# Sharing the square root, inverse and offset of two layer norms, and dividing half of the heads on ScalarE, in the combine stage of a graph network kernel

## The reference

```python
msgs = jnp.where(deg[:, None, None] > 0, agg, V)      # agg: weighted sums over a node's edges, each head over its denominator
out = msgs.reshape(N, H * D) @ Wo + bo
x1 = out + node_features
gnn = (x1 - mean(x1)) / jnp.sqrt(var(x1) + 1e-05) * gamma + beta
x = x + gnn + mix(xn)                                 # mix ends in a product with Wproj
x = x + ffn(layernorm(x))                             # the gate of ffn takes the second norm's rows
```

## Time and profile before

| | us |
|---|---|
| median of 3 runs | 1252.35 (1250.92, 1252.35, 1252.89) |
| the profiled execution, whole | 1250.91 |
| its span | 1249.2 |
| DVE in the combine: its first instruction to the gate's bias | 826.77 to 944.61 |

### The profile page before, as it was taken

How to read it: one execution, slowest core, us unless ns; L and a number is a source line. 1 busy time by engine, 2 the same in 40 slices (tenths; PEclk the granted TensorE clock), 3 DMA queues, 4 the chain that set the end, 5 groups by cost and what they waited for, 6 DMA issues and landing times. The chain is left out here.

```text
span 1249.2 us, 26412 instructions
## 1 busy us (share of the span) xinstructions
PE 1095.1 (88%) x7190; PEld 842.0 (67%) x7191; DVE 919.0 (74%) x1987; ACT 814.8 (65%) x2874; POOL 803.1 (64%) x835
## 2 busy tenths in 40 slices
PE   4999957999999999999999999968883599999992
PEld 3777734666767666767767676657872588888872
DVE  7787548899999999999999999859876323223230
ACT  3445400788888889898988888614673456666661
POOL 4777657777777777777777777117541356666661
PEclk9999965899999999999999999979995799999997
DMA  8333368888888888888888888258125633343444
GB/s 233 123 126 125 128 162 245 241 241 240 241 234 247 237 242 234 237 240 244 238 243 239 242 240 238 69 174 291 64 92 161 200 52 60 66 64 62 67 64 120
DMA packets 131578, 220.51 MB, mean 177 GB/s; under 512 B 24900, under 2 KB 89580, under 8 KB 131400
## 3 DMA queue, kind: packets, MB, share of 16 engines
q0 software_dynamic: 48832, 138.49, 41.3%
q1 hardware_dynamic: 82632, 80.63, 20.9%
HBM read 188.00 MB, written 34.25 MB: 178 GB/s over the span
## 5 line engine op out<-in xcount | busy, mean ns | idle before, releaser
L640 POOL DMA_INDIRECT KV<-kv,ixs x464 | 477.7, 1030 | 148.5 <-issue 135.6
L656 ACT ACTIVATE KV<-KV,WS 128x65 f32<-128x65 f32 x1728 | 434.0, 336 | 17.9 <-ACT RR L702 14.8
L769 PE MATMUL ps_o<-KV,PM 128*128 128x260 f32 x928 | 252.8, 395 | 20.3 <-DVE PM L888 13.9
L750 PE MATMUL ps_qe<-Q,PT 128*128 x1392 | 201.6, 284 | 5.6 <-DVE PT L856 5.1
L769 PEld LDWEIGHTS ps_o<-KV,PM 128*128 128x128 f32 x928 | 158.8, 190 | 60.6 <-DVE PM L888 29.1
L750 PEld LDWEIGHTS ps_qe<-Q,PT 128*128 128x128 bf16 x1392 | 137.1, 100 | 52.9 <-issue 10.1
L774 PE MATMUL ps_o<-ACC,ident 128*128 x464 | 158.5, 423 | 0.6 <-ACT ACC L682 0.6
L877 DVE TENSOR_TENSOR KV<-KV,ps_qe 128x512 f32<-128x512 f32 x232 | 149.8, 677 | 0.2
L870 DVE TENSOR_TENSOR KV<-KV,ps_u 128x1024 f32<-128x1024 f32 x116 | 140.3, 1209 | 8.8 <-DMA KV<-kv,ixs 8.8
L1547 POOL DMA_INDIRECT acc<-YG,DX x56 | 89.2, 1593 | 79.2 <-issue 49.0
L883 DVE TENSOR_REDUCE S<-KV 128x16 f32<-128x1024 f32 x116 | 138.8, 1197 | 1.1
(11 more groups left out here) (298 smaller groups left out, 1655.2 us busy)
## 6 DMA issues: line engine op xcount, KB each, us to landing
dlb<-dl_rows SPq DMA_DIRECT2D x116, 128.0 KB
W<-in_f_W_dram SPq DMA_DIRECT2D x16, 512.0 KB, 6.4
tyb<-ty_rows SPq DMA_DIRECT2D x116, 64.0 KB
KV<-kv,ixs POOLq DMA_INDIRECT x464
kv<-kvb SPq DMA_DIRECT2D x25, 258.0 KB, 2.4
xs_rows<-xs SPq DMA_DIRECT2D x25, 256.0 KB, 2.5
VB<-kv SPq DMA_DIRECT2D x5, 650.0 KB, 8.2
X<-in_x_dram SPq DMA_DIRECT2D x5, 640.0 KB, 10.8
```

Source lines behind the costliest of these rows:

```text
L640: pool.indirect_dma_start(kv[:, c % KR, n, :], None, d["kv"], bass.IndirectOffsetOnAxis(ap=T["ixs"][:, c % KR, n:n + 1], axis=0)).then_inc ...
L656: m = a.activation(part, part, ACT.Copy, scale=W[:, c % 2, s * H + h:s * H + h + 1])
L750: m = pe.matmul(T["ps_qe"][:, p % 3, k, :], T["PT"][:, h, (p % 2 * 2 + k) * P:(p % 2 * 2 + k + 1) * P], T["Q3"][:, bass.ds(at + n * C, C)] ...
L769: m = pe.matmul(T["ps_o"][:, p % RO, 0:A], PM[:, p // 2 % 2, p % 2 * 2 + k, :], kv[:, c % KR, 2 * x + k, C:KVW], start=(k == 0), stop=False)
```

## The change

Three things, all in the combine.

- Pass j has one square root, one inverse and one offset for both norms: of tile j for the first norm and of tile j - 4 for the second. The statistics move to tables indexed by pass (`mv2`, `rs2`, `nm2`: NT + 4 passes by two norms), so that one instruction takes both as two elements of a row. For passes that have one norm only it takes one element (`norms`). `deviations` waits for both variances.
- DVE's `message` takes heads 0 and 1 (128 elements a row). ACT gets a `message` for heads 2 and 3, two copies of 128x64 with a scale per row, issued last in its pass; those of tiles 0 and 1 come ahead of everything. PE's turn waits for both halves (`s_ma`).
- ACT's copies of tile 0 wait for `first_messages` on a semaphore of their own (`s_fm`).

```diff
+    s_fm, s_ma = sem("cb_first_sums"), sem("cb_messages_by_scalar")
...
+    NSTEP = NT + ST2
+
+    def norms(j):
+        return slice(0 if j < NT else 1, 2 if j >= ST2 else 1)
...
+    HV = 2
...
             def message(t):
                 wait(v, s_pv, 2 * (t // CT_))
-                v.tensor_tensor(VB[:, t, 0:C].rearrange("p (h d) -> p h d", h=H), acc3[:, t, :].rearrange("p (h d) -> p h d", h=H)[:, :, 0:D],
-                                dn[:, t, :].unsqueeze(2).broadcast_to([P, H, D]), ALU.mult).then_inc(s_ms, 1)
+                v.tensor_tensor(VB[:, t, 0:HV * D].rearrange("p (h d) -> p h d", h=HV), acc3[:, t, :].rearrange("p (h d) -> p h d", h=H)[:, 0:HV, 0:D],
+                                dn[:, t, 0:HV].unsqueeze(2).broadcast_to([P, HV, D]), ALU.mult).then_inc(s_ms, 1)
...
+            def inverse(j):
+                v.wait_ge(s_dv, j + 1)
+                note(v.reciprocal(T["rs2"][:, j, norms(j)], T["rs2"][:, j, norms(j)]), "rs", j)
+
+            def offset(j):
+                noted("rs", j)
+                v.scalar_tensor_tensor(out=T["nm2"][:, j, norms(j)], in0=T["mv2"][:, j, norms(j), 0], scalar=-1.0, in1=T["rs2"][:, j, norms(j)],
+                                       op0=ALU.mult, op1=ALU.mult).then_inc(s_rc, 1)
...
+            def deviations(j):
+                if j < NT:
+                    a.wait_ge(s_sq1, j + 1)
+                if j >= ST2:
+                    a.wait_ge(s_sq2, j - ST2 + 1)
+                a.activation(T["rs2"][:, j, norms(j)], T["mv2"][:, j, norms(j), 1], ACT.Sqrt, bias=T["eps"][:, 0:1]).then_inc(s_dv, 1)
...
+            def message(t):
+                if t == 0:
+                    a.wait_ge(s_fm, 1)
+                wait(a, s_pv, 2 * (t // CT_))
+                for h in range(HV, H):
+                    m = a.activation(VB[:, t, h * D:(h + 1) * D], acc3[:, t, h * (D + 1):h * (D + 1) + D], ACT.Copy, scale=T["dn"][:, t, h:h + 1])
+                m.then_inc(s_ma, 1)
+            message(0)
+            message(1)
             turned(0)
...
-                if 0 <= i - 1 < NT:
-                    deviation(i - 1, 0, s_sq1, s_a1)
-                if 0 <= i - AG2 < NT:
-                    deviation(i - AG2, 1, s_sq2, s_a2)
+                if 0 <= i - 1 < NSTEP:
+                    deviations(i - 1)
+                if i + 2 < NT:
+                    message(i + 2)
...
             def turn(i):
                 pe.wait_ge(s_ms, i + 1)
+                pe.wait_ge(s_ma, i + 1)
                 pe.wait_ge(s_as, i + 1)
```

More of the change, by code:

```diff
@@ L1026, in phase_combine @@
          "empty_nodes", "empty_added", "messages", "mix_scaled"))
-    s_am, s_t, s_tc, s_pr, s_q, s_sq1, s_a1, s_rc1, s_yn, s_yg, s_res, s_sq2, s_a2, s_rc2, s_xf, s_xt, s_gt, s_gc, s_gp, s_e = (sem("cb_" + n) for n in
-        ("mix_products", "turned", "turned_copied", "products", "residual_added", "variance", "deviation", "inverse_deviation", "normed",
-         "scaled", "residuals", "second_variance", "second_deviation", "second_inverse_deviation", "second_normed", "rows_stored",
+    s_fm, s_ma = sem("cb_first_sums"), sem("cb_messages_by_scalar")
+    s_am, s_t, s_tc, s_pr, s_q, s_sq1, s_dv, s_rc, s_yn, s_yg, s_res, s_sq2, s_xf, s_xt, s_gt, s_gc, s_gp, s_e = (sem("cb_" + n) for n in
+        ("mix_products", "turned", "turned_copied", "products", "residual_added", "variance", "deviations", "inverse_deviations", "normed",
+         "scaled", "residuals", "second_variance", "second_normed", "rows_stored",
          "gate_turned", "gate_copied", "gate_products", "gate_exponents"))
@@ L1032, in phase_combine @@
     NC_ = NT // CT_
-    INV, ST2, AG2, INV2, GL = 2, 4, 5, 6, 7
+    INV, ST2, GL = 2, 4, 7
+    NSTEP = NT + ST2
+    def norms(j):
+        return slice(0 if j < NT else 1, 2 if j >= ST2 else 1)
     s_vt, s_xr = ([sem(f"cb_{n}{c}") for c in range(NC_)] for n in ("v_rows", "q_and_residual_rows"))
@@ L1179, in variance @@
                 noted("stats", norm, t)
[L1180 to L1189, removed]
+                v.bn_aggr(T["mv2"][:, t + ST2 * norm, norm, :], T["stats2"][:, norm, t % 2, :]).then_inc(signal, 1)
+            def inverse(j):
[5 more added lines that the diff above has]
+                                       op0=ALU.mult, op1=ALU.mult).then_inc(s_rc, 1)
             first_messages()
@@ L1195, in _ @@
                 scale_mix(t)
-            for i in range(NT + INV2 + 1):
+            for i in range(NSTEP + INV):
                 if i + 2 < NT:
                     mix_sums(i + 2)
[L1199 to L1202, removed]
+                if i >= INV:
+                    inverse(i - INV)
                 if i + 2 < NT:
@@ L1205, in _ @@
                     scale_mix(i + 2)
[L1206 to L1209, removed]
+                if i >= INV:
+                    offset(i - INV)
                 if 0 <= i - 1 < NT:
                     variance(i - 1, 0, s_sq1)
-                if 0 <= i - AG2 < NT:
-                    variance(i - AG2, 1, s_sq2)
+                if 0 <= i - 1 - ST2 < NT:
+                    variance(i - 1 - ST2, 1, s_sq2)
                 if i < NT:
@@ L1278, in _ @@
                     scale_row(i - INV)
-                if 0 <= i - INV2 < NT:
-                    second_norm(i - INV2)
-                if 0 <= i - 1 < NT:
-                    deviation(i - 1, 0, s_sq1, s_a1)
-                if 0 <= i - AG2 < NT:
-                    deviation(i - AG2, 1, s_sq2, s_a2)
+                if 0 <= i - INV - ST2 < NT:
+                    second_norm(i - INV - ST2)
+                if 0 <= i - 1 < NSTEP:
+                    deviations(i - 1)
+                if i + 2 < NT:
+                    message(i + 2)
             a.wait_ge(s_e, 1)
```

16 lines of the change are left out of this document (7 added, 9 removed).

## The result

The changed kernel is slower: a median of 1256.97 us (10 runs, 1251.47 to 1264.32) against 1251.19 for the kernel before, run beside it (10 runs, 1250.76 to 1252.89), a ratio of 1.0052 with a 95% interval of 1.0037 to 1.0068. The forecast was 1257.5. Its runs spread over 13 us where those of the kernel before spread over 2, and the profiled execution, 1263.27 us, is one of the long ones. So I took a second profile of each kernel (1257.47 and 1250.36 us), and read the differences from all four.

The account below looks back on a forecast made before the run. The matmul engine bounds the combine, except at three pairs of long GpSimd additions, where VectorE's held instructions do. 2.5 + 0.6 + 2.8 + 0.2 = +6.1 us on 1250.91 gives 1257.0; forecast 1257.5, range 1251.5 to 1259.5.

Parts of the forecast that it names:

- Steady steps: Later row-tile steps of the combine: the matmul engine still sets 3.28 us a step, so the change adds 0.
- the loop of 3.22: Wait loop through VectorE, ScalarE's copies and the matmul engine: 3.22 us a step with the second norm, under 3.28.
- The two copies: ScalarE's half of the message, two copies at the end of its pass: 0.59 us for the pair.
- The new wait at the first pair: First pair of long GpSimd additions: turn waits for ScalarE's copies behind the held offset, +1.4, fallen clock +1.1: +2.5 us.
- The toss at its start: First pair, other end: VectorE's message starts 0.05 us behind GpSimd's addition and is not held, -0.9 us instead of +2.5.
- Steps 3 to 6: Three early row-tile steps of the combine: 8.30 us become 3 x 2.97 = 8.90, +0.6 us.
- Second pair: Second pair of long GpSimd additions: message falls inside the first, costing 5.3 instead of 2.5, +2.8 us; other end 0.
- Third pair: Third pair of long GpSimd additions: turn at 891.03 already waited for the second norm, copies end at 891.2, +0.2 us.
- Start and tail: First messages and the steps after tile 22: 0, give or take 0.4 us.
- Inverse held: VectorE's two-element inverse, if held like the offset, adds up to 0.5 us; taken as 0.
- Rival 2: VectorE's shorter step puts its message first at all three pairs of GpSimd additions: -3.1 us, 1247.8; chance 0.08.
- Rivals 1 and 3: 1: first-pair message beats GpSimd, second pair unchanged, 1251 to 1252.5, chance 0.12; 3: ScalarE bounds steady steps, up to 1259.5, 0.05.

Follow-up runs that it names:

- the split alone: Kernel before with the message cut between VectorE and ScalarE, root, inverse and offset left separate, two load semaphores joined: 1259.4 us, ratio 1.0067.
- the kernel with the unheld offset: Changed kernel with the offset as two one-element operations, each with one SBUF tensor and a scalar per row: 1246.59 us, 0.9958 of before.

## Why the prediction was right, and where it was not

- *Steady steps, 0:* right. The seven steps from tile 14 on take 3.28 us, and the wait grew by what VectorE saved. That the loop of 3.22 was close to the bound showed in the split alone, which passes it.
- *The two copies, 0.59:* 0.57 in the rows. From the release of the offset to the end of the copies 1.30 us were forecast and 1.29 measured (854.51 to 855.80).
- *The new wait at the first pair, +2.5:* right in place and kind, shown by moving the copies ahead and by freeing the offset. Too small by 1.1 as the mean of two profiles: 0.4 of it lies ahead of the offset's release (in the second profile, the message of 2.04 us), 0.7 behind it. The step that failed is the price of the fallen clock, put at a fixed 1.1 us from one stretch, the third pair of the kernel before, where turn to addition took 3.49 and the clock came back within the product (1.73 and 1.03 us). Here it took 4.54 (855.90 to 860.44) in one profile and 3.90 (855.42 to 859.32) in the other, and 2.39 in the split alone. Against the 2.35 that the prediction counted without a fallen clock, the same stand of 3.10 us cost 2.2, 1.6 and nothing.
- *The toss at its start, −0.9:* it did not fall so in the two profiles of the change (the message came 0.17 and 0.35 us behind the addition). In the kernel with the unheld offset it did, 0.01 us behind, and the message ran in 0.27.
- *Steps 3 to 6, +0.6:* 0.64 and 0.24 over the mean of before: right in the first profile, less in the second.
- *Second pair, +2.8:* right, the message fell inside the first addition (870.86 after 870.60; in the second profile 869.34 after 869.28). Of the 0.6 above it 0.3 is the clock in the mean, as turn to addition took 4.08 us (877.87 to 881.95) and 3.58 (876.55 to 880.13) against 3.49; 0.2 lies ahead of the turn.
- *Third pair, +0.2:* 0.9. The copies did not delay the turn; from tile 11 to the turn it took 8.34 us (891.79 to 900.13) against 8.37 before. It is all the clock: turn to addition took 4.54 and 4.53 against 3.49 and 3.78 in the two profiles of before.
- *Start and tail, 0:* +0.5 in the mean: 0.27 is the step from tile 21 to 22 (3.15 us against 2.88), the rest the step behind the third pair (3.75 and 3.37 against 3.28); neither was tested.
- *Inverse held, up to 0.5:* no inverse was held, as taken.
- *Rival 2, faster by the order at the starts:* it did not come; against GpSimd's first addition VectorE's message came later than before, not earlier: 0.26 behind it at the second pair where it had been 0.56 ahead, and 0.40 behind at the third (893.26 after 892.86) where it had been 0.27. Rivals 1 and 3 did not come either.

So the mechanism was right and one term was mis-sized, the clock after a stand: it makes some 2 of the 2.8 us by which the combine of the profiled executions lost more than forecast (8.9 instead of 6.1). That the median rose by 5.8, near the 6.1, owes something to luck: executions without a profile lost less, there or elsewhere, than those that I could read, and where is not shown.

## What to carry to other kernels

Before a piece of work moves to another engine, look at what stands ahead of it in that engine's program: here the moved half stood behind an instruction which waits for one that is held, and so a 2.6 us hold on VectorE that had cost little at the first pair became a wait of the matmul engine there, mostly with a fallen clock on top, and the delay moved the next message into the next addition. Taking work off an engine that waits was worth nothing here. What paid was to end the hold itself, by cutting the long additions and by an operation with one tensor in SBUF, and that was there to be had in the kernel before.

## What the runs showed of the hardware

- The form of an operation of one element decides whether it is held. Minus mean times inverse took 2.62 us inside a long addition with both inputs as tensors in SBUF, and 0.20 with one of them as the scalar per row. The Trainium skill (SBUF — State Buffer, Who interferes with whom) says that a VectorE instruction with at most one SBUF input, outside the two-port modes, does not contend with GpSimd; the row at 847.29 agrees.
- A message that started 0.01 us behind GpSimd's addition was not held (0.27 us at 846.77), like the one 0.05 behind in the earlier trace rows; one that started 0.06 behind was (2.45 us at 869.34), like all those further behind. The two that were not held came with a longer addition (2.50 and 2.63 us against 2.36). The Trainium skill (the same section) gives the ports to whichever issues first; by the starts in the rows those two went the other way, and the one 0.06 behind agrees.
- After stands of 2.8 to 3.1 us the matmul engine's clock mostly fell to the 1.2 GHz level (granted 0.50), but for different times: the product that followed ran as 1.73 + 1.03 and 1.92 + 1.19 us at the third pair in the two profiles of the kernel before, and as 1.91 + 1.91, 1.91 + 1.71, 1.91 + 1.27 or 1.80 + 1.03 in those of the changed one. In the split alone it ran as 1.03 + 1.03 after 3.10 us, at a granted clock of 1.00. With the unheld offset it ran as 1.92 + 1.82 (at 854.79) after two shorter stands, of 1.28 and 0.69 us. What decides between them no run here shows.
